# An attention and feed-forward block: small ScalarE copies ahead of the softmax seeds, two row groups normalised on another engine, a reordered tail, and idle products at the start

## The reference

```python
def _L0_attn_ref(x, Wq, bq, Wk, bk, Wv, bv, Wo, bo):      # H = 16 heads of HD = 64
    q = jnp.einsum('bsd,dhk->bshk', x, Wq) + bq
    k = jnp.einsum('bsd,dhk->bshk', x, Wk) + bk
    v = jnp.einsum('bsd,dhk->bshk', x, Wv) + bv
    q = q / jnp.sqrt(jnp.asarray(depth, q.dtype))
    attn = jax.nn.softmax(jnp.einsum('bqhd,bkhd->bhqk', q, k), axis=-1)
    out = jnp.einsum('bhqk,bkhd->bqhd', attn, v)
    return jnp.einsum('bqhd,hdm->bqm', out, Wo) + bo
def _L0_ffn_ref(x, U1, V1, b1, U2, V2, b2):               # rank 32, 512 hidden
    P = jnp.einsum('bsd,dr->bsr', x, U1)
    H = jax.nn.gelu(jnp.einsum('bsr,rf->bsf', P, V1) + b1)
    Q = jnp.einsum('bsf,fr->bsr', H, U2)
    return jnp.einsum('bsr,rd->bsd', Q, V2) + b2
x = x + _layernorm(_L0_attn_ref(_layernorm(x), ...))
x = x + _layernorm(_L0_ffn_ref(_layernorm(x), ...))
```

## Time and profile before

| | us |
|---|---|
| median of 3 runs | 2408.31 (2408.15 to 2410.71) |
| the profiled execution | 2408.61 |
| its span | 2406.8 |
| PE busy | 2363.3 (98%) |
| ACT busy | 2140.5 (89%) |
| DVE busy | 2044.8 (85%) |
| POOL busy | 2033.3 (84%) |
| granted clock of TensorE, mean | 0.994 |

### The profile page before, as it was taken

The page is one execution under the profiler, slowest core; times in us unless marked ns, Lnnn a source line. Parts: engine busy times, 40 slices in busy tenths (PEclk is TensorE's granted clock), DMA queues, the critical chain, the costliest instruction groups (busy, mean ns, idle before and its releaser), DMA issues.

```text
span 2406.8 us, 44126 instructions
## 1 busy us (share of the span) xinstructions
PE 2363.3 (98%) x15628; PEld 1158.0 (48%) x15628; DVE 2044.8 (85%) x3249; ACT 2140.5 (89%) x2427; POOL 2033.3 (84%) x1141
## 2 busy tenths in 40 slices
PE   6999999999999999999999999999999999999998
PEld 3444444445445454444445444454444545444444
DVE  7888888888888888888888888888888888888977
ACT  5999999898998999999998999999999998989976
POOL 4888888888888888888888888888888888889986
PEclk8999999999999999999999999999999999999999
DMA  1100001000000000100001000100000000110101
GB/s 51 28 15 28 28 15 33 28 14 28 28 20 28 28 14 28 34 15 27 28 15 33 28 15 27 33 21 22 28 27 21 28 27 15 35 29 21 36 27 36
DMA packets 62973, 62.59 MB, mean 26 GB/s; under 512 B 28868, under 2 KB 46660, under 8 KB 62756
## 3 DMA queue, kind: packets, MB, share of 16 engines
q1 hardware_dynamic: 61748, 59.44, 8.3%
q10 hardware_dynamic: 1008, 0.33, 0.1%
HBM read 56.88 MB, written 2.61 MB: 25 GB/s over the span
## 4 chain that ended last, share of the span: by engine, by line
PE 92%; DVE 3%; POOL 2%; ACT 2%; issue 1%; DMA 0%; POOLq 0%; ACTq 0%; DVEq 0%
PE o_ps L428 35%; PE spare_ps L390 13%; PE score_ps L407 11%; PE score_ps L410 9%; PE score_ps L413 9%; PE spare_ps L376 3%; PE spare_ps L367 3%; PE spare_ps L358 3%; PE spare_ps L473 3%; POOL total L1113 2%; PE spare_ps L440 1%; DVE max_part L838 1%; ACT probs L664 1%; ACT score_ps L654 0%; DVE ln_stats L804 0%
## 5 line engine op out<-in xcount | busy, mean ns | idle before, releaser
L1113 POOL TENSOR_TENSOR total<-total,probs 128x832 f32<-128x832 f32 (+1 forms) x896 | 1761.9, 1966 | 294.1 <-ACT probs L664 216.9
L838 DVE TENSOR_REDUCE max_part<-spare_ps 128x1 f32<-128x512 f32 x2027 | 1302.2, 684 | 310.5 <-PE spare_ps L390 294.4
L664 ACT ACTIVATE probs<-score_ps 128x1024 f32<-128x1024 f32 x1024 | 993.7, 1023 | 219.1 <-PE score_ps L413 217.0
L654 ACT ACTIVATE score_ps<-m_all 128x1024 f32<-128x1024 f32 x1024 | 1012.1, 1032 | 14.4 <-DMA m_all<-m_scratch 14.4
L428 PE MATMUL o_ps<-probs,v_sb 128*64 128x512 f32 x4096 | 974.9, 597 | 0.0
L428 PEld LDWEIGHTS o_ps<-probs,v_sb 128*64 128x64 f32 x4096 | 271.5, 137 | 423.5 <-issue 278.3
L390 PE MATMUL spare_ps<-k_hi,q_hi 64*128 64x512 f32 x2027 | 455.8, 445 | 11.7 <-DVE max_part L838 8.3
L407 PE MATMUL score_ps<-q_hi,k_hi 64*128 64x512 f32 x2048 | 426.9, 413 | 1.2 <-ACT score_ps L654 1.2
L413 PE MATMUL score_ps<-q_hi,k_lo 64*128 64x512 f32 x2048 | 405.3, 391 | 0.0
L410 PE MATMUL score_ps<-q_lo,k_hi 64*128 64x512 f32 x2048 | 404.7, 391 | 0.0
L390 PEld LDWEIGHTS spare_ps<-k_hi,q_hi 64*128 64x128 f32 x2027 | 194.1, 184 | 424.4 <-issue 239.8
(11 more groups left out here) (131 smaller groups left out, 926.4 us busy)
## 6 DMA issues: line engine op xcount, KB each, us to landing
m_all<-m_scratch SPq DMA_DIRECT2D x64, 512.0 KB, 4.3
denom<-denom_scratch SPq DMA_DIRECT2D x122, 128.0 KB, 2.9
m_scratch<-neg_rows SPq DMA_DIRECT2D x256, 1.0 KB
y_acc<-in_L_attn_x SPq DMA_DIRECT2D x8, 256.0 KB, 5.9
xg<-in_L_attn_x SPq DMA_DIRECT2D x8, 256.0 KB, 2.8
block_out<-probs SPq DMA_DIRECT2D x8, 256.0 KB, 2.3
denom_col<-denom SPq DMA_DIRECT2D x61, 4.0 KB
denom_scratch<-denom_col SPq DMA_DIRECT2D x61, 4.0 KB, 1.4
```

The source lines that it names most:

```text
L654: nc.scalar.activation(score_ps[st % 2][:], m_all[:, G % 2], ACT.Copy).then_inc(s["seed_done"], 1)
L664: nc.scalar.activation(probs[:, st % RING], score_ps[st % 2][:], ACT.Exp, scale=SCALE).then_inc(s["exp_done"], 1)
L838: nc.vector.reduce_max(max_part[:, G % 2, h, qt, kc:kc + 1], bank[max_bank(n, h)], AX.X).then_inc(s["max_done"], 1)
L1113: nc.gpsimd.tensor_tensor(others(total[:, G % 2], G), so_far, others(probs[:, st % RING], G), ALU.add).then_inc(s["sum_done"], 1)
```

## The change

- `act_xn_columns` and `act_low_rank` go ahead of the two seeds instead of behind them, in all steps of `XT` and `P_AT`.
- `LATE_T1` goes from 5 to 7: groups 5 and 6 are normalised by ScalarE (`act_t1`, behind the seeds of steps 504 and 510) and no longer by VectorE; GpSimd then computes a shift as well for them (two more instructions each). The steps of groups 4 to 6 in the tables move by up to two.
- For chunk 62, `column_denominators` and `head_projections` go from steps 505 and 506 to 506 and 507.
- The remainder of V1 (`dve_v1`) goes from step 488 to step 509 on VectorE.
- Behind step 511: TensorE takes the last column sums and `hidden(1)` ahead of `xn_columns(6)`, and `second_rank(7)` ahead of `outputs(6)`. VectorE takes group 7's normalising, adding and statistics ahead of `dve_z(0)`, and `dve_xn(7)` ahead of `dve_z(1)`. GpSimd does `pool_r2(6)` behind its last sums, then `pool_r1(7)`, `pool_r2(7)`, and then waits for `dve_xn(7)` before it begins `pool_r3(0)`.
- `keep_clock(6)`: at the head of step 0 six products of 512 columns into bank `o`, whose results nobody reads.

```diff
-COLUMNS_AT = {8 * (CHUNKS - 2) + 3: CHUNKS - 3, 8 * (CHUNKS - 1) + 1: CHUNKS - 2}
+COLUMNS_AT = {8 * (CHUNKS - 2) + 3: CHUNKS - 3, 8 * (CHUNKS - 1) + 2: CHUNKS - 2}
...
-T1 = [470, 478, 486, 494, 502, 503, 508]
+T1 = [470, 478, 486, 494, 502, 504, 510]
...
-LATE_T1 = 5
+V1_AT = 509
+
+LATE_T1 = NG - 1
...
+            def keep_clock(self, times):
+
+                ps = self.take("o", None, 0)
+                for _ in range(times):
+                    nc.tensor.matmul(ps, q_hi[:, 0, 0:P], k_hi[:, 0, 0:CH], start=True, stop=True)
...
             for n in range(DOUBLES):
                 G, u, c, d = n // PER_CHUNK, n // (PER_CHUNK * NC), n // PER_CHUNK % NC, n % PER_CHUNK
+                if n == 0:
+                    me.keep_clock(6)
...
             me.values(STEPS - 1)
-            me.xn_columns(6)
             me.column_denominators(CHUNKS - 1)
             me.hidden(1)
+            me.xn_columns(6)
             me.head_projections(CHUNKS - 1)
...
             me.second_rank(6)
+            me.second_rank(7)
             me.outputs(6)
-            me.second_rank(7)
             me.outputs(7)
...
                     act_q(act, G + 2)
+                for g in ffn_at(n, XT):
+                    act_xn_columns(act, g)
+                for g in ffn_at(n, P_AT):
+                    act_low_rank(act, g)
                 if n + 1 < DOUBLES:
                     act_seed(act, 2 * n + 2)
                     act_seed(act, 2 * n + 3)
...
             act_o(act, CHUNKS - 1)
+            act_hidden(act, 1)
             act_xn_columns(act, 6)
-            act_hidden(act, 1)
...
+        def dve_v1(dve):
+            dve.wait_ge(f["v1_high"], 1)
+            nc.vector.tensor_tensor(v1_third, v1_f32[2 * RANK:SPLIT], v1_third.bitcast(F32), ALU.subtract).then_inc(f["v1_split"], 1)
...
             dve_low(dve, 6)
-            dve_z(dve, 0)
             dve_t1(dve, 7)
             dve_x1(dve, 7)
             dve_st2(dve, 7)
+            dve_z(dve, 0)
+            dve_xn(dve, 7)
             dve_z(dve, 1)
-            dve_xn(dve, 7)
...
+            pool_r2(pool, 6)
             pool_r1(pool, 7)
+            pool_r2(pool, 7)
+
+            pool.wait_ge(f["f_xn"], NG)
             pool_r3(pool, 0)
             pool_scale(pool, 0)
-            pool_r2(pool, 7)
             pool_out(pool, 0)
```

31 lines of the change are left out of this document (13 added, 18 removed).

## The result

The change takes 2413.28 us (median of 20 runs, 2409.84 to 2415.09) against 2408.26 us for the kernel before on the same chip: ratio 1.0018, 95% interval 1.0011 to 1.0025. The forecast was 2409.2 with a range of 2405.5 to 2412.2, so the time lies above the range, 4 us above the forecast. The 20 times fall in two groups, which the explanation needs: three of 2409.8 to 2410.6, and the rest from 2412.1 up, most of them near 2413.3. The profiled execution is one of the latter: 2413.37 us, span 2411.6. All 20 executions are in the chip's fast state, so the groups lie within it.

What follows compares the result with a forecast made beforehand. TensorE was taken as the bound up to step 500, ScalarE from 503. Attention 1.0 earlier, `dve_head_y` 0.5 earlier, then 0.9 lost at the end: span 2406.8 to 2407.7, median 2408.31 to 2409.2; range 2405.5 to 2412.2.

Steps and rivals of the forecast that it cites:

- The clock: Behind step 511: the sum let TensorE's clock hold, with `dve_head_y` at 2369.0, 0.5 earlier than before.
- its own rival, at 25%: Behind step 511: TensorE's clock falls after 1.9 us idle ahead of the last column sums, end up to 2411.9; chance 25%.
- The rival's price: Fall behind step 511: last sums 2.48 instead of 1.84, later products doubled, 2.7 in all up to `dve_head_y`.
- The end behind `xn(7)`: GpSimd starts `out(3)` 14.9 after `xn(7)` and holds up `dve_out(4)`; 0.9 lost at the end.
- the new order: GpSimd's and VectorE's changed order behind step 511: 1.4 more from `dve_head_y` to the end, 38.7 for 37.3.
- The end of attention: Step 511's exponentials: 0.6 gained by the last steps, attention 1.0 earlier with the other terms, at 2357.8.
- the stall: TensorE's wait of 2.08 at step 505's column sums goes; step 507 comes 3.3 earlier.
- ScalarE's new work: Last steps: copies out of ScalarE's wait and `t1(6)` take 1.6 and 1.1 of the 3.3 gained.
- the late copies: From step 504, ScalarE's copies ahead of the seeds are no longer hidden in its wait: 1.6 lost.
- Steps 480 and 488: Copies ahead of the seeds lose 0.4 at 480; V1's remainder leaving 488 gains 1.0.
- The start: Six idle products ahead of the first scores: between 0.9 gained and 1.0 lost, taken as 0.2 lost.
- the rival at 5%: Idle products don't raise the clock and step 506's sums stall as before: 2411 to 2414; chance 5%.

Runs made afterwards that it cites:

- e16: The change with the last column sums 64 columns wide and eight idle TensorE products in the wait ahead of them: 2411.44 us, 2.3 over before.
- e2: The change without the six idle products at the start: 2411.50 us, 2.9 over before.
- e13: The kernel before, unchanged, timed and traced a second time: 2408.98 us; its profiled execution 2410.45 us.
- e18: The kernel before with all three column sums 64 columns wide: 2408.12 us, 0.1 over before.
- e1: The change with eight idle TensorE products in the wait ahead of the last column sums: 2410.93 us, 2.3 over before.
- e9: The change with the last column sums 64 columns wide instead of one: 2411.70 us, 2.3 over before.
- e6: e3 with GpSimd's and VectorE's order behind step 511 as in the kernel before: 2409.18 us, 0.2 over before.
- e4: The kernel before with only chunk 62's column sums and head projections one step later: 2406.24 us, 2.4 below before.
- e5: The change with `t1` of groups 5 and 6 back on VectorE and the groups' steps as before: 2409.56 us, 0.6 over before.
- e10: e4 with the last column sums 64 columns wide and ScalarE's copies ahead of the seeds at all steps: 2407.11 us, 2.3 below before.
- e12: e4 with the last column sums 64 wide, copies ahead up to step 499 and GpSimd's `out(3)` behind `r3(5)`: 2406.90 us, 2.5 below before.
- e14: e12 with the remainder of V1 moved on VectorE from step 488 to 509: 2403.87 us, 5.3 below before, ratio 0.9979.
- e3: The change with VectorE's statistics of group 6 behind the four last additions instead of ahead: 2411.62 us, 3.0 over before.

## Why the forecast was wrong, by its steps

- **The clock.** The forecast's sum let it hold behind step 511, and its own rival, at 25%, let it fall. That choice is the step that failed: from step 511 to `dve_head_y` the change takes 15.1 for the 11.2 of the sum, and e16, where it holds, 11.15. The choice rested on "against it, the idle part is a little shorter" (1.9 against 2.08 us in step 505). The wait was 2.22, and the runs show that so small a difference decides nothing. Whether the clock falls, when and for how long differs from one execution to the next: behind the same wait of 2.22 and the same sums it fell ahead of them and for 10.2 us in the change's trace, behind them and for 3.4 us in e2's. With a wait of 0.76, 6 of 11 times are of the upper group, with wide sums and 2.2 2 of 11. At the place from which the forecast took its rule, step 505, it fell in all three traces that have the wait (2.08 in before, 1.84 in e13, 2.02 in e18), and 1.84 is shorter than the 1.9 that was to speak against a fall. The question was not whether but how often.
- **The rival's price** was also too small: 2.7, where the fall cost 3.9 in the profiled execution. I took the sums at 2.48, from a row of before in which the clock fell half way through; with the clock down from their start they take 3.54 for 1.84, 1.7 more where the rival had 0.6. `hidden(1)`, the transposes and the head projections cost 0.85, 0.45 and 0.95 more, much as the rival had them; all four together make about 3.9.
- **How much of the median that is.** In the profiled execution, all of the 3.9. For the median, the kernels that fill TensorE's wait (e1), widen the last sums (e9) or do both (e16) all stay 2.3 over before, so 2.7 of the 5.0 hang on what TensorE does ahead of and in the last sums. The forecast was 0.9 over before; the 1.4 between stay open. The fall at step 499 is one part in e16's trace, but 2 traces of 18 are too few to put the whole on it.
- **The end behind `xn(7)`** was right in the profiled execution. GpSimd has no gap from 2384.00 to `out(3)` at 2398.88, 14.9 as forecast, and `dve_out(4)` needs 2.13 beside it for 1.10. The Trainium skill, SBUF — State Buffer, section "SBUF: two separate sides", has the loser wait for the whole instruction. By that rule the trace agrees within 0.2: 1.03 longer, with 1.20 of `out(3)` still to run. What the new order costs in all the forecast had too small, 1.4 for 2.3 (e6), as its rows of before held a fall of the clock.
- **The end of attention** was hit, 2357.83 for 2357.8, and in part by luck. Two terms were both too small and partly cancel: the stall was worth 4.6 for 3.3 (e4), and ScalarE's new work took 3.5 for 2.7 (e5), with `t1` at 2.7 and the late copies at 0.9, where I had 1.1 and 1.6. The rest of the error cancels against the base, below.
- **Steps 480 and 488**: 0.5 lost for 0.4 (9.95 against 9.46 from step 480's to step 482's exponentials), 1.3 gained for 1.0 (9.76 against 11.02 over two steps), of which 0.3 had gone at step 487 (4.45 against 4.18), a term that I had at nothing. The gain belongs to the move of V1, as e10, e12 and e14 show; the copies without it lose 2.
- **The start**: six products, 2.93 us, full speed before 47. From the pair of maxima near 42 to the seeds of step 1 it takes 6.99 (e1 6.79, e3 6.84) against 6.70: 0.1 to 0.3 lost for 0.2.
- **The base.** The traced execution of before was 0.7 early at step 481 against its second trace (e13), and the change's own trace stands there where that second one does (2214.57 and 2214.53). The forecast had no margin for it. It is no part of the 3.9, but it is what makes step 511 come out to 0.03: with it away, the change's attention would have ended 0.7 before the forecast.

Where the clock holds, the forecast's distances are met (e16, 49.8 for 49.9). The three fastest of the change's 20 times, 2409.8 to 2410.6, have a mean granted clock of 0.995 over the execution, the profiled one 0.993, and e3's trace without a fall 0.995. So they are likely to be executions without the long fall, but none of them was traced, and e1's trace (2410.05) shows that a time of this size can hold a short one. The measured time also lies where the rival at 5% put it (2411 to 2414), by nothing of what that rival said: the idle products brought the clock up, and the sums of chunk 62 did not wait. The ratio of 1.0018 is still within 0.2%, at its very edge. The range ended at 2412.2 because the rival's price set it.

## What to carry to other kernels

When a forecast hangs on whether TensorE's clock falls, look at many times of the kernel before, not at one trace: groups in them can be outcomes of one place, and a small edit can move the share of each and with it the median. A row taken from one trace can hold such a fall, as did the 37.3 behind `dve_head_y`. Price the fall from its earliest point, at half clock for all that is on the chain. And a stall that goes is worth only what its neighbours don't take: put nothing new on the engine that is the bound of the steps behind it.
